# A routed feed-forward kernel on one core: the x turn of tile 6, the place of two pieces of vector work, and the bank of token chunk 4

## What is computed

```python
y = x @ W_base.T + (((x @ Wt.T) @ A[idx].T) @ B_w[idx].T) @ Wp.T * scaling[idx]   # 2048 rows
probs = softmax(y @ gate_w.T)                    # 16 experts
w, e = top_k(probs, 2); w = w / (w.sum() + 1e-20)
out = x + sum_k w[k] * (silu(y @ w_gate[e[k]].T) * (y @ w_up[e[k]].T)) @ w_down[e[k]].T   # 352 wide
```

## Time and profile before

| | |
|---|---|
| median of 3 runs | 344.13 us (341.58 to 346.34) |
| profiled execution | 343.24 us, span 341.3 us |
| TensorE busy | 332.0 us, 97% |
| VectorE, ScalarE, GpSimd busy | 234.1, 179.5, 121.0 us (69%, 53%, 35%) |
| mean granted TensorE clock | 0.995 of full |
| chain that ended last | 93% TensorE, 3% transfers, 2% ScalarE |
| transfers | 82.45 MB; one expert's weights are 1408 and 768 KB, four copies xs<-xg of 64 KB make one tile |

### The profile page before, as it was taken

One profiled execution on the slowest core, in us unless ns is written; L12 is line 12 of the kernel. 1 busy time (PEld: TensorE's weight loads), 2 busy tenths in 40 slices (PEclk: granted clock), 3 DMA queues, 4 the chain that ended last, 5 costly groups with the idle time before them and its releaser, 6 DMA issues.

```text
span 341.3 us, 7490 instructions
## 1 busy us (share of the span) xinstructions
PE 332.0 (97%) x1847; PEld 292.8 (86%) x1847; DVE 234.1 (69%) x310; ACT 179.5 (53%) x246; POOL 121.0 (35%) x85
## 2 busy tenths in 40 slices
PE   7999999998999999999999999999999999999993
PEld 5647688878999999999998998999999999999981
DVE  4438699898555576594878848779677579879310
ACT  4157934622546455636547555675545575585221
POOL 0000000021443743246574553537425371344323
PEclk9999999999999999999999999999999999999997
DMA  7957596947599799999999999998999969721144
GB/s 278 408 233 285 154 437 213 323 154 271 167 361 351 156 327 323 251 327 201 267 297 342 312 274 310 209 307 267 226 342 193 336 125 294 152 27 28 12 63 61
DMA packets 47924, 82.45 MB, mean 242 GB/s; under 512 B 5552, under 2 KB 22576, under 8 KB 47792
## 3 DMA queue, kind: packets, MB, share of 16 engines
q1 hardware_dynamic: 38912, 62.96, 55.4%
q0 software_dynamic: 8960, 18.89, 26.8%
HBM read 60.58 MB, written 19.92 MB: 236 GB/s over the span
## 4 chain that ended last, share of the span: by engine, by line
PE 93%; DMA 3%; ACT 2%; issue 1%; POOLq 0%; SPq 0%
PE bank L706 46%; PE bank L735 25%; PE bank L680 4%; PE bank L570 3%; PE bank L571 3%; PE bank L572 3%; PE bank L491 3%; PE bank L454 2%; DMA x_st<-xin 2%; DMA lead_sb<-lead 1%; PE bank L608 1%; PE bank L623 1%; PE bank L580 1%; ACT lt_sb L790 1%; POOLq L96 0%
## 5 line engine op out<-in xcount | busy, mean ns | idle before, releaser
L1280 POOL DMA_INDIRECT out<-ys,sidx x40 | 73.0, 1825 | 122.7 <-DMA out<-ys,sidx 68.2
L706 PE MATMUL bank<-w_hi,xt_hi 128*128 x320 | 82.1, 333 | 1.2 <-ACT y_st L801 1.2
L1259 POOL DMA_INDIRECT xg<-y_rows,gidx x40 | 47.4, 1186 | 94.7 <-DMA y_rows<-y_st 76.7
L353 DVE TENSOR_TENSOR w_lo<-w_raw,w_hi (+2 forms) x32 | 76.2, 2382 | 5.5 <-issue 3.0
L706 PE MATMUL bank<-w_hi,xt_lo 128*128 x320 | 79.1, 324 | 0.0
L706 PE MATMUL bank<-w_lo,xt_hi 128*128 x320 | 79.0, 323 | 0.0
L351 ACT ACTIVATE w_hi<-w_raw (+2 forms) x32 | 64.7, 2021 | 4.2 <-DMA w_raw<-wall 2.4
L870 ACT ACTIVATE sg<-bank 128x352 f32<-128x352 f32 x40 | 18.5, 464 | 79.6 <-PE bank L706 79.4
L706 PEld LDWEIGHTS bank<-w_hi,xt_hi 128*128 128x128 f32 x320 | 54.6, 189 | 2.3 <-issue 1.6
L706 PEld LDWEIGHTS bank<-w_lo,xt_hi 128*128 128x128 f32 x320 | 56.1, 189 | 0.1
L706 PEld LDWEIGHTS bank<-w_hi,xt_lo 128*128 128x128 f32 x320 | 56.1, 189 | 0.0
(11 more groups left out here) (184 smaller groups left out, 366.6 us busy)
## 6 DMA issues: line engine op xcount, KB each, us to landing
w_raw<-wall SPq DMA_DIRECT2D x16, 1408.0 KB
w_raw<-wall SPq DMA_DIRECT2D x16, 768.0 KB
xs<-xg SPq DMA_DIRECT2D x132, 64.0 KB
y_rows<-y_st SPq DMA_DIRECT2D x16, 256.0 KB, 6.5
x_st<-xin SPq DMA_DIRECT2D x6, 512.0 KB, 12.9
lead_sb<-lead SPq DMA_DIRECT2D x4, 512.0 KB, 5.2
head_sb<-head SPq DMA_DIRECT2D x2, 640.0 KB, 8.4
wb_sb<-wb SPq DMA_DIRECT2D x2, 512.0 KB, 11.0
```

The lines of the kernel that those rows point to most:

```text
L353: e.tensor_tensor(lo, raw, hi, ALU.subtract).then_inc(own, 1)
L706: mm = e.matmul(bank[2 + 2 * s + t % 2][:, 0:INTER], a, w[:, bass.ds(at + (k * GU + s * INTER), INTER)], start=k == 0 and i == 0, stop=k = ...
L1259: e.indirect_dma_start(out=xg[t % NXG][:], out_offset=None, in_=y_dram, in_offset=bass.IndirectOffsetOnAxis(ap=gidx[:, t:t + 1], axis=0)). ...
L1280: e.indirect_dma_start(out=out, out_offset=bass.IndirectOffsetOnAxis(ap=sidx[:, t:t + 1], axis=0), in_=ys[t % NYS][:], in_offset=None, bou ...
```

## The change

There are four edits. `N_PE` goes from 7 to 6, so tile 6 too is turned by copies and VectorE. `AT_TURN` goes from (4, 0) to (4, 1), and chunk 4 (`NYST`) is made in bank 7 instead of bank 0, a bank that held logits: its first three matmuls stand ahead of the logits turn, and wait for the readers of bank 7 instead of for `y_stage`. `weigh(0)` moves from ahead of the first gate-up subtractions to behind `y_low(0)`. The subtraction of the first down weights moves from behind the third one-hot to behind `product(0)`.

```diff
--- before.py
+++ after.py
@@ -71,10 +71,10 @@
 WARM = 256
 N_WARM0 = 16
 C_WORDS, C_LOAD, C_AT_BY, C_SPLIT = 8, 7, 9, 10
-AT_TURN, AT_RANKS, AT_TABLES, AT_NEED, AT_X = (4, 0), (6, 2), (12, 3), (13, 0), (CH - 1, 2)
+AT_TURN, AT_RANKS, AT_TABLES, AT_NEED, AT_X = (4, 1), (6, 2), (12, 3), (13, 0), (CH - 1, 2)
 NYST = 4
 NXG, NYS = 8, 4
-N_PE, NXS = 7, 4
+N_PE, NXS = 6, 4
 N_LEAD, N_COPY, N_SOON = 9, 6, 3
 T_RETIRE = (NFULL + 3, NFULL + 9)
 Q = 32
@@ -226,6 +226,7 @@
         bank = [ctx.enter_context(nc.psum_tensor(f"bank{i}", [P, 512], F32)) for i in range(8)]
         qs_bank = [bank[i] for i in (4, 6, 4, 6)]
         lg_bank = [bank[i] for i in (6, 7, 4, 5)]
+        y_bank = [lg_bank[1] if c == NYST else bank[c % 4] for c in range(CH)]
         g_ps = bank[4][:].rearrange("p (k b n) -> p k b n", k=KH, n=NEXP)
         y_dram = nc.dram_tensor("y_rows", [NTOK, H], F32, kind="Internal").ap()
 
@@ -563,13 +564,18 @@
 
             def y_base(c, ks):
                 b, r = divmod(c, CPB)
-                e.wait_ge(a_y, c - 3)
+                if c == NYST:
+                    e.wait_ge(a_lt, 2)
+                    e.wait_ge(a_z, 3)
+                    e.wait_ge(v_z, 2)
+                else:
+                    e.wait_ge(a_y, c - 3)
                 for k in ks:
                     hi, lo = (v[b][:, k, r * P:(r + 1) * P] for v in (x_hi, x_lo))
                     e.wait_ge(v_xlo, x_halves(b, k // 2 + 1))
-                    e.matmul(bank[c % 4][:], hi, w_base_hi[:, k], start=k == 0, stop=False, skip_group_check=True)
-                    e.matmul(bank[c % 4][:], hi, w_base_lo[:, k], start=False, stop=False, skip_group_check=True)
-                    e.matmul(bank[c % 4][:], lo, w_base_hi[:, k], start=False, stop=False, skip_group_check=True)
+                    e.matmul(y_bank[c][:], hi, w_base_hi[:, k], start=k == 0, stop=False, skip_group_check=True)
+                    e.matmul(y_bank[c][:], hi, w_base_lo[:, k], start=False, stop=False, skip_group_check=True)
+                    e.matmul(y_bank[c][:], lo, w_base_hi[:, k], start=False, stop=False, skip_group_check=True)
 
             def y_rank(c):
 
@@ -577,7 +583,7 @@
                 e.wait_ge(a_qs, NBATCH)
                 e.wait_ge(a_z, 2 * (b + 1))
                 e.wait_ge(v_z, b + 1)
-                e.matmul(bank[c % 4][:], z_stack[0:ZK, b, r * P:(r + 1) * P], q_stack[0:ZK, b],
+                e.matmul(y_bank[c][:], z_stack[0:ZK, b, r * P:(r + 1) * P], q_stack[0:ZK, b],
                          start=False, stop=True, skip_group_check=True).then_inc(m_y, 1)
 
             def ranks():
@@ -798,7 +804,7 @@
                 e.wait_ge(m_y, c + 1)
                 if c >= NYST:
                     e.wait_ge(d_y[c % NYST], 16 * (c // NYST))
-                e.activation(y_st[c % NYST][:], bank[c % 4][:], ACT.Copy).then_inc(a_y, 1)
+                e.activation(y_st[c % NYST][:], y_bank[c][:], ACT.Copy).then_inc(a_y, 1)
 
             def x_evac(t):
                 with in_use(e, count, t):
@@ -1149,9 +1155,6 @@
 
             softmax_second()
             token_weights()
-            e.wait_ge(v_w12, 1)
-            weigh(0)
-            e.wait_ge(v_chain, done[0])
 
             count = tile_count(e)
             half = PARTS["gu"][1] // 2
@@ -1193,14 +1196,16 @@
                     e.tensor_tensor(hh[t % 2][:], sg[t % 2][:], bank[4 + t % 2][:, 0:INTER], ALU.mult).then_inc(v_h, 1)
 
             y_low(0)
+            e.wait_ge(v_w12, 1)
+            weigh(0)
             weigh(1)
             e.wait_ge(v_chain, done[0])
             e.tensor_tensor(where, where, wide(w_part[2][:]), ALU.mult).then_inc(v_ohq, 1)
-            split_weights(e, count, 0, None, "dn", v_dn)
             word = tile_word(e, 1)
             split_weights(e, count, 1, word, "gu", v_gu)
             y_low(1)
             product(0)
+            split_weights(e, count, 0, None, "dn", v_dn)
             e.wait_ge(m_tb, 2)
             step(e.tensor_copy(wtab[:], bank[7][:, 2 * TQ:3 * TQ]))
             step(e.tensor_tensor(wtab[:], wtab[:], bank[7][:, TQ:2 * TQ], ALU.add))
```

## The result

The changed kernel took 348.82 us (median of four runs, 347.71 to 350.39); the kernel before, run beside it, 343.13 us (341.58 to 346.34). The ratio is 1.0203, with a 95% interval from 1.0158 to 1.0247: slower, by 7 us and so by just about the 2% that divides the forecast's cases; on which side of 2% it lies the interval leaves open. The two medians differ by less, 5.7 us; they are taken over all executions, the ratio only over those that were not in the slower state that the same program shows at times. The two profiled executions differ by 7.15 us. The direction and the place were forecast; the size was not: 3.5 us were forecast, and a loss of over 2% had a chance of 0.06 only.

A forecast was written before the change was run, and what follows sets the result against it. TensorE, busy 332.0 of 341.3 us, was taken as the bound. Turn -0.35, first tile -0.6, transposes -0.45, stall +3.4 and clock +1.5 made +3.5 us on 343.24, so 346.8 us, range 342 to 350.5.

The forecast's parts named there:

- Chunk 4 ahead of the turn: Before the logits turn: three matmuls fill a 0.63 us wait; gain 0.65, about 0.3 back at the ranks, 0.35 us carried.
- weigh(0) behind y_low(0): First tile: gate_up(0) starts 1.17 us earlier, the turn's 0.35 included; about 0.2 goes back at the tables, 0.95 remain.
- Down weights behind product(0): VectorE, first tile: the 1.75 us subtraction moved ahead of the weight table and h_low(0) costs nothing.
- Four transposes: Tile 6: four transposes leave TensorE, saving 0.45 us; TensorE would so be 1.4 us ahead.
- Stall at down(4): Tile 6's copies and turn delay h_low(4); down(4) starts at 118.2 instead of 114.8, a 3.4 us stall.
- Clock: After the stall TensorE's clock falls and matmuls run at half pace; 1.5 us taken, bounds 0 and 3.88.
- Sum: All terms together: -0.35 -0.6 -0.45 +3.4 +1.5 = +3.5 us, giving 346.8 us.
- Stall, but no fall of the clock: Rival: stall ahead of down(4) with the clock staying full; +2.0 us, 345.2 us; chance 0.27.
- The gains stay: Rival: h_low(4) ends before 114.8, so no stall; 341.8 us; chance 0.15 with the transposes rule and cases between.
- Slower by over 2%: Rival: clock stays at half for over a tile, 6.31 us more; 351.5 us; chance 0.06.
- point of decision: In the case of over 2% slower: it decides from 4.9 us of lost matmul time.
- My last sentence: Closing sign: slower than forecast if xs copies end the gap before down(4) at over 5, or the clock stays low.

The follow-up runs named there:

- e9: e1 with the logits turn ahead of chunk 4 again (AT_TURN at (4, 0)), chunk 4 still in bank 7; 347.74 us, measured once, not comparable in time.
- e1: Changed kernel with tile 6 back on TensorE (N_PE 7), the other three edits kept; 342.3 us, ratio 0.9988 to the kernel before.
- e5: Changed kernel with SP issuing the copies of tiles 6 and 7 ahead of the fourth expert's weights; 346.8 us, ratio 1.0089.
- e4: Changed kernel with 50 unused matmuls of 256 columns on TensorE between gate_up(5) and down(4), filling the gap; 346.76 us, ratio 1.0129.
- e12: e2 with the rank matmuls one k-step later, at (6, 3); copies where the change has them; 342.64 us, ratio 1.0003.
- e11: Changed kernel with tile 6 on TensorE (N_PE 7) and the rank matmuls at (6, 3); 343.18 us, ratio 1.0014.
- e3: Changed kernel with SP issuing tile 6's four copies ahead of the fourth expert's weights; 349.68 us, ratio 1.0216.
- e7: e2 with the copies of tiles 6 and 7 issued ahead of the fourth expert's weights, as in e5; 346.27 us, ratio 1.0092.
- e8: e7 with the rank matmuls one k-step later in chunk 6, at (6, 3); 345.32 us, ratio 1.0064.
- e2: Changed kernel with tile 6's turn moved from pass 4 to pass 5 on ScalarE and VectorE, copies unmoved; 343.48 us, ratio 1.0007.
- e10: Kernel before with N_PE 6 alone, so only tile 6 moves to copies and VectorE; 350.25 us, ratio 1.0222.
- e6: Changed kernel with, on ScalarE, the high part of tile 5's down weights ahead of tile 6's xt_hi; 344.7 us, ratio 1.0046.

## Why the prediction was right and wrong

- **Chunk 4 ahead of the turn.** Right in mechanism: the wait is gone, and one of 0.43 us came before the second rank matmul (0.3 forecast). The term was too large: at most 0.2 by e9 against e1, where 0.35 was carried, and no more than the spread of kernels that are the same up to there.
- **weigh(0) behind y_low(0).** Right: gate_up(0) came 1.29 us ahead (1.17 forecast). What goes back at the tables was less than I said: 1.21 of the 1.29 are left at gate_up(2), where the forecast had 0.95.
- **Down weights behind product(0).** Costs nothing, as forecast: no gap at down(0), and gate_up(2) keeps its lead.
- **Four transposes.** 0.49 us, 0.45 forecast: from gate_up(2) to gate_up(5) the kernels with tile 6 on VectorE take 20.10 or 20.11 us, those with it on TensorE 20.57 to 20.62. In all TensorE was 1.70 us ahead, where 1.4 was said.
- **Stall at down(4).** The chain was right link by link, and its length too. From the landing of tile 6's copies to down(4) I walked 118.2 - 110.6 = 7.6 us; it took 120.54 - 113.07 = 7.47. The 2.8 us that I gave for copies that aren't late are 2.59 in e5. The step that failed is the landing, the moment from which the copies are signalled as complete: "Tile 6's take their place, so they land near 110.6", with 4.4 us of stall only "if they land a microsecond later than I say". The copies were usable at 113.07, 2.5 us later. That one number makes the stall 5.79 instead of 3.4. I took the landing from the end of the packets in SP's queue, and that can't be done: the 14 packets of half a microsecond were a lull, and a few packets can be the ones that are waited for. In the changed kernel SP's issues, and its packets, MB and share from 111.5 to 112, look the same:

```profile
101.88 14.02 SPq L429 DMA_DIRECT2D xs<-xg  x16
...
q1 hardware_dynamic: 15, 0.01, 8.2%
```

The packed traces answer it, though no printed view lists it: they hold the increments of each semaphore. That of tile 6's copies in the changed kernel has 45 recorded increments (some can be missing), 42 of them from 106.82 to 110.90, and then three at 112.49, 112.67 and 112.86; the turn starts 0.21 us after the last. So most parts of the copies were there about when I said, and a few came 2 us behind. In the kernel before, tile 7's copies, whose place tile 6's took, have their last increment at 113.19, not near 111.5. The first turn there stood at 117.19 and never waited, so it did not show. With 113.19 less 0.95, and the 7.6 us that I walked from the landing, down(4) would have come at 119.8 and the stall would have been forecast at 5.0 us. Why these parts are late stays open.

- **Clock.** The mechanism was right, and the term too small: 2.6 us (e4) where 1.5 was taken between 0 and 3.88. I had argued that part of the half-clock time would lie in the stall. It did for 1.1 of 6.8 us: the clock fell 4.7 us into the idle time. That it fell "some 2 us into the idle time" was what the earlier trace rows showed at the end of the kernel; here it was 4.7.
- **Sum.** -1.7 us (-1.4 forecast), +6.0 from gate_up(5) to down(4) (5.79 of it the gap; 3.4 forecast), +2.7 from there to gate_up(7) against the kernel before (1.5 forecast): +7.0 where I had +3.5.
- **The rivals.** "Stall, but no fall of the clock" fell with the windows above. "The gains stay" fell with the gap; "Slower by over 2%" came far nearer than its 0.06 (whether it came true the interval leaves open), but not by its mechanism: the clock was at half for 5.8 us of work, under one tile, and cost 2.6 us, not 6.3; the copies did the rest. I had its point of decision, 4.9 us, but no case in which late copies and the clock came together: they were both tied to a landing at 110.6. My last sentence, slower "if xs copies end it at over 5, or the clock stays low", came nearest; I gave it no share of the 0.06.

The Trainium skill's rule on transposes ("VectorE: DVE Perf Modes", section "Rules for kernel authors") would have kept tile 6 on TensorE. That is the better choice with the order of this change, but not for the price that I worked out from it: the four transposes are worth the 0.49 us that they take, and the loss is one of order and transfers. With the turn in pass 5 it is not (e12 against e11).

**What the copies do when SP's order is changed.** The Trainium skill ("DMA: Bandwidth & Descriptors", section "Queues, rings and completion order") says that every DMA engine takes turns only between the queue rows for which it has work. Copies and weights are in one queue here, so by that rule nothing lets a small copy past a large weight transfer that was issued earlier; e3, e5, e7 and e8 agree: whichever tile's copies were left behind the weights was the one whose turn waited (4.34, 4.15, 3.99 and 3.27 us).

**What stays open.** e1, e2, e11 and e12 are 1.0 to 2.0 us ahead of the kernel before at gate_up(7), and their ratios (0.9988, 1.0007, 1.0014, 1.0003) show none of it; 1.5 us would be 0.9955, just outside the intervals of e11 and e12 (from 0.9971 and 0.9961). In single traces part of the lead is given back between gate_up(7) and the end of the last down: before, after, e3, e4 and e10, which have no lead, take 210.9 to 211.1 us for it, those that are ahead 211.1 (e1), 211.5 (e12), 211.8 (e11), 212.6 (e2) and 214.6 (e9). But the lead is not all of it: e5, e7 and e8 are behind the kernel before at gate_up(7) and take 212.0 too, and e6, also behind, 211.2. Where time is lost, turns wait for copies (2.76 us at 270.76 in e2, with the gap of 0.89 us behind it; 3.27 at 130.33 in e11). The DMA engines are near full there in the changed kernel (windows, columns as above):

```profile
126.50:310.00 183.50, 183.50 (x1049) 170.23 (x1048) 135.95 (x141) 104.85 (x140) 84.75 (x55) 1.00 0.95 251
```

That the transfers take the lead back in the timed runs would fit this, but it is only argued: each kernel has one trace, and even there e12 keeps 1.51 us to the end. No version beat the kernel before; e12 and e11 are faster than the changed one by about 2%, and no more.
